# Summing counted edge blocks directly into a ring of three weight tiles, in place of running sums and their differences

## What is computed

```python
# layer 2 (x is already scaled by deg^-1/2)
msg = x[src]
agg = jax.ops.segment_sum(msg, dst, num_segments=h.shape[0])
...
# layer 3 (a self loop is added to the edges)
out = jax.ops.segment_sum(norm[:, None] * h[src], dst, num_segments=N) + b
```

## Time and profile before

| what | us |
|---|---|
| median of 3 timed runs | 4976.39 (4974.26 to 4980.61) |
| the profiled execution, whole | 4979.84 |
| its span, first to last instruction | 4977.6 |
| TensorE busy | 4160.5 (84%) |
| VectorE busy | 2661.7 (53%) |
| ScalarE busy | 1549.6 (31%) |
| GpSimd busy | 1840.2 (37%) |
| mean granted TensorE clock | 0.919 |

### The profile page before, as it was taken

How to read it: one execution, slowest core, us unless ns; L and a number is a source line. 1 busy time by engine, 2 the same in 40 slices (tenths; PEclk the granted TensorE clock), 3 DMA queues, 4 the chain that set the end, 5 groups by cost and what they waited for, 6 DMA issues and landing times. The chain is left out here.

```text
span 4977.6 us, 70703 instructions
## 1 busy us (share of the span) xinstructions
PE 4160.5 (84%) x21605; PEld 3198.6 (64%) x21605; DVE 2661.7 (53%) x5828; ACT 1549.6 (31%) x3042; POOL 1840.2 (37%) x1628
## 2 busy tenths in 40 slices
PE   4899995864917999889999668997799999979978
PEld 2565653643715666568888657886687767768855
DVE  4588888888138999836665560002433322233354
ACT  0233331011314333345565324443001333310023
POOL 0477773872446767536666402113100000000011
PEclk9899997986968999999999879998899999999989
DMA  1599994830845666647666419996423000022200
GB/s 66 177 286 287 295 281 141 260 98 26 264 145 166 181 181 182 190 149 204 184 180 170 138 44 338 323 323 189 122 74 88 1 1 1 2 82 77 61 14 26
DMA packets 519774, 748.78 MB, mean 150 GB/s; under 512 B 80123, under 2 KB 438273, under 8 KB 519301
## 3 DMA queue, kind: packets, MB, share of 16 engines
q1 hardware_dynamic: 405810, 490.95, 31.9%
q0 software_dynamic: 62656, 189.33, 13.8%
q10 hardware_dynamic: 50960, 64.09, 3.7%
HBM read 526.98 MB, written 217.19 MB: 150 GB/s over the span
## 5 line engine op out<-in xcount | busy, mean ns | idle before, releaser
L2828 PE MATMUL sum_ps<-table_rows,block_weights 128*125 128x256 f32 x2500 | 564.7, 386 | 37.1 <-DMA table_rows<-k_table 37.1
L2828 PEld LDWEIGHTS sum_ps<-table_rows,block_weights 128*125 128x125 f32 x2500 | 465.6, 189 | 136.2 <-issue 70.2
L109 POOL DMA_INDIRECT rows_all<-kv_table,src_of_visit x416 | 445.1, 1070 | 221.6 <-issue 111.8
L2632 POOL TENSOR_TENSOR window_sums<-window_sums,brought_blocks 128x650 f32<-128x650 f32 x320 | 427.8, 1337 | 223.6 <-ACT running_blocks L2642 140.2
L2521 POOL DMA_INDIRECT gathered_rows<-k_table,src_of_chunk x392 | 409.2, 1044 | 208.4 <-issue 113.9
L2743 PE MATMUL sum_ps<-gathered_rows,hit 128*126 x1376 | 364.6, 390 | 22.6 <-DVE window_sums L2709 19.0
L2810 DVE TENSOR_TENSOR block_weights<-raw 128x625 f32<-128x625 uint16 x248 | 183.6, 805 | 349.7 <-PE sum_ps L2828 323.6
L2570 PE MATMUL block_ps<-cell_hot,low_hot 128*128 128x325 bf16 x1280 | 231.8, 304 | 141.5 <-DVE cell_hot L2560 140.4
L2057 DVE TENSOR_TENSOR y<-out_ps,b 128x256 f32<-128x256 f32 x120 | 51.0, 425 | 553.0 <-PE out_ps L1956 553.0
L3327 POOL MEMSET eps<- 125x1 f32 x1 | 0.1, 98 | 917.8 <-POOLq L2770 917.8
L2579 ACT ACTIVATE block_copies<-block_ps 128x650 bf16<-128x650 f32 x320 | 227.9, 712 | 358.1 <-PE block_ps L2570 356.7
(11 more groups left out here) (500 smaller groups left out, 8245.8 us busy)
## 6 DMA issues: line engine op xcount, KB each, us to landing
w<-in_L_ffn_W SPq DMA_DIRECT2D x112, 1024.0 KB, 7.5
v_kept<-rows_all SPq DMA_DIRECT2D x104, 512.0 KB, 5.0
v_rows<-v_kept SPq DMA_DIRECT2D x104, 512.0 KB, 4.5
visit_blocks<-block_copies ACTq DMA_DIRECT2D x320, 162.5 KB, 2.9
brought_blocks<-visit_blocks SPq DMA_DIRECT2D x320, 162.5 KB, 3.3
blocks<-running_blocks SPq DMA_DIRECT2D x320, 162.5 KB, 3.5
raw<-blocks SPq DMA_DIRECT2D x250, 162.5 KB, 2.2
w<-in_L_ffn_w SPq DMA_DIRECT2D x64, 256.0 KB, 3.7
```

What stands on the lines that cost most here:

```text
L109: pool.indirect_dma_start(env.ring[:, k % KEPT_RING, i, :], None, env.kv_table, bass.IndirectOffsetOnAxis(env.src_of_visit[:, k * VB + i:k ...
L2632: pool.tensor_tensor(self.totals[:, k % 2, :], self.totals[:, (k - 1) % 2, :], self.brought[:, k % self.BROUGHT, :], ALU.add).then_inc(sel ...
L2828: mm = pe.matmul(sum_ps[0:P, t % banks, 0:D], weights[0:k, t % floats, h, :], rows[0:k, h, :], start=h == 0, stop=h == BH - 1)
```

## The change

The running sums are gone from the attention phase. In each later sum SyncE now brings all 320 counted bf16 blocks in order, eight in flight, and VectorE adds each block in place to the 25 columns of its window in one of three f32 weight tiles: `here * same + block`, where `same` is 1 if the visit has the same window as the one before and 0 if a window begins (so the old contents are dropped). Which tile and which columns, VectorE reads from packed words, one for four visits, that setup now makes with a vector `block_same`; the address of each addition is worked out in registers. TensorE waits for the number of visits up to the end of its tile (`visits_upto`). In the second sum ScalarE copies the result to `part`, and GpSimd adds it. The attention's two kinds of small transfers move from ScalarE's list to SyncE's, one of its tiles gets a buffer of its own, and 17 groups instead of 15 stay in SBUF.

```diff
 setup_phase
-                done(v.tensor_scalar(env.block_last[0:1, 0:BC - 1], bank[6][0:1, 1:BC], -1.0, None, ALU.add))
-                done(v.memset(env.block_last[0:1, BC - 1:BC], BV - 1))
+                done(v.tensor_copy(env.visits_upto[0:1, 0:BC - 1], bank[6][0:1, 1:BC]))
+                done(v.memset(env.visits_upto[0:1, BC - 1:BC], BV))
+                done(v.memset(block_same[:, 0:1], 0.0))
+                done(v.tensor_tensor(block_same[:, 1:BV], tile_bc[1][:, 1:BV], tile_bc[1][:, 0:BV - 1], ALU.is_equal))
+                divided(block_tile, 205, 10)
+                divided(block_lap, 137, 11)
...
 relation_attention_phase
-        running = RunningBlocks(env, st, ph, carve(2 * BX))
...
-                running.sync(sp)
+                for g in range(NS):
+                    if g < NS - KEPT:
+                        bring_back(g)
+                    sp.wait_ge(o_made, g + 1)
+                    n = windows_of(g) * WN
+                    sp.dma_start(env.o_table[g * SW * WN:g * SW * WN + n, :], o_rows[g % 2][0:n, :]).then_inc(stored[g % 2], 16)
...
-                running.gpsimd(pool)
...
-                    exps(g)
-                    running.scalar(act)
+                    exps(g)
...
 dense_sum_phase
-                    at = sp.value_load(env.block_last[0:1, w:w + 1], min_val=0, max_val=BV - 1)
-                    sp.dma_start(raw[:, w % raws, :], env.blocks[ds(at, 1)].rearrange("o p n -> p (o n)")).then_inc(raw_landed[w % raws], 16)
+                    if n >= raws:
+                        sp.wait_ge(added, n - raws + 1)
+                    sp.dma_start(raw[:, n % raws, :], env.visit_blocks[n]).then_inc(raw_landed[n % raws], 16)
...
-                        if w == 0:
-                            ins = v.tensor_copy(block_of, upto(w))
-                        else:
-                            ins = v.tensor_tensor(block_of, upto(w), upto(w - 1), ALU.subtract)
-                        ins.then_inc(converted, 1)
+                v.memset(weights[:, 0], 0.0).then_inc(cleared, 1)
+                v.wait_ge(cleared, 2)
+                v.wait_ge(same_landed, 16)
+                for g in range(BV // BGROUP):
+                    word = v.value_load(env.block_words[0:1, g:g + 1], min_val=1 << 5 * BGROUP, max_val=(T + 1 << 5 * BGROUP) - 1)
+                    laps = [((word >> (5 * i + 3)) & 3).with_bounds(min_val=0, max_val=floats - 1) for i in range(BGROUP)]
+                    places = [((word >> (5 * i)) & 7).with_bounds(min_val=0, max_val=per_tile - 1) for i in range(BGROUP)]
+                    v.wait_ge(multiplied, (word >> (5 * BGROUP)).with_bounds(min_val=1, max_val=T))
+                    for i in range(BGROUP):
+                        n = g * BGROUP + i
+                        v.wait_ge(raw_landed[n % raws], 16 * (n // raws + 1))
+                        if n > 0:
+                            v.wait_ge(added, n)
+                        here = weights[:, ds(laps[i], 1), :, ds(places[i], 1), :].rearrange("p f h o d -> p (f h) (o d)")
+                        v.scalar_tensor_tensor(out=here, in0=here, scalar=same[:, n:n + 1],
+                                               in1=raw[:, n % raws, 0:BH * BW].rearrange("p (h d) -> p h d", h=BH),
+                                               op0=ALU.mult, op1=ALU.add).then_inc(added, 1)
...
+                    upto = pe.value_load(env.visits_upto[0:1, last:last + 1], min_val=1, max_val=BV)
...
+                    pe.wait_ge(added, upto)
...
+                pool.memset(weights[:, 1:floats], 0.0).then_inc(cleared, 1)
+                if onto:
+                    for t in range(T):
+                        pool.wait_ge(taken, t + 1)
+                        pool.tensor_tensor(sums[0:P, t, :], sums[0:P, t, :], part[:, t % 2, :], ALU.add).then_inc(onto_made, 1)
```

More of the change, by code:

```diff
@@ L56 @@
 BCHUNKS = 2
+FLOATS = 3
+BGROUP = 4
 BV = QUADS * (CHUNKS // BCHUNKS) + BC - 1
@@ L2589, in all_stored @@
             act.wait_ge(self.stored[s], 16 * len(range(s, beyond, self.COPIES)))
[L2592 to L2643, removed]
@@ L2762, in dense_sum_phase @@
         rows = sb(env, st, "table_rows", [128, BH, D])
-        raw = sb(env, st, "raw", [128, raws, BX], U16)
-        weights = sb(env, st, "block_weights", [128, floats, BH, P])
+        raw = sb(env, st, "raw", [128, raws, BX], BF16)
+        weights = sb(env, st, "block_weights", [128, floats, BH, per_tile, BW])
+        same = sb(env, st, "block_same", [128, BV])
+        part = sb(env, st, "part_sums", [P, 2, D])
         sum_ps = ps(env, st, "sum_ps", [128, banks, 512])
@@ L2767, in dense_sum_phase @@
         rows_landed = [ph.sem() for _ in range(G + 1)]
-        converted, multiplied, taken = [ph.sem() for _ in range(3)]
+        cleared, same_landed, added, multiplied, taken, onto_made = [ph.sem() for _ in range(6)]
         parts = [(j * G, min(whole, (j + 1) * G)) for j in range(G)]
@@ L2786, in _ @@
                 sp.dma_start(rows[0:N - whole * 128, whole, :], table[whole * 128:N, :]).then_inc(rows_landed[G], 16)
-                for w in range(per_tile, BC):
-                    bring(w)
+                for n in range(raws, BV):
+                    bring(n)
             @block.vector
             def _(v):
-                def upto(w):
-                    return raw[:, w % raws, 0:BH * BW].rearrange("p (h d) -> p h d", h=BH)
-                def take(t):
-                    v.wait_ge(multiplied, t + 1)
-                    here = sums[0:P, t, :]
-                    v.tensor_tensor(here, here, sum_ps[0:P, t % banks, 0:D], ALU.add).then_inc(taken, 1)
@@ L2800, in _ @@
-                for t in range(T):
-                    if t >= floats:
-                        v.wait_ge(multiplied, t - floats + 1)
-                    for i in range(per_tile):
-                        w = t * per_tile + i
-                        v.wait_ge(raw_landed[w % raws], 16 * (w // raws + 1))
-                        block_of = weights[:, t % floats, :, i * BW:(i + 1) * BW]
-                        if w == 0:
-                            ins = v.tensor_copy(block_of, upto(w))
-                        else:
-                            ins = v.tensor_tensor(block_of, upto(w), upto(w - 1), ALU.subtract)
-                        ins.then_inc(converted, 1)
-                    if onto and t >= floats:
-                        take(t - floats)
@@ L2814, in _ @@
-                if onto:
-                    for t in range(T - floats, T):
-                        take(t)
+                v.memset(weights[:, 0], 0.0).then_inc(cleared, 1)
[15 more added lines that the diff above has]
+                                               op0=ALU.mult, op1=ALU.add).then_inc(added, 1)
@@ L2827, in _ @@
                         k = 128 if h < whole else N - whole * 128
-                        mm = pe.matmul(sum_ps[0:P, t % banks, 0:D], weights[0:k, t % floats, h, :], rows[0:k, h, :], start=h == 0,
+                        mm = pe.matmul(sum_ps[0:P, t % banks, 0:D], weights[0:k, t % floats, h].rearrange("p i d -> p (i d)"), rows[0:k, h, :], start=h == 0,
                                        stop=h == BH - 1)
@@ L2956, in relation_attention_phase @@
     with ExitStack() as st:
-        parts = [carve(2 * SW * WR) for _ in range(4)]
+        parts = [carve(2 * SW * WR) for _ in range(3)] + [sb(env, st, "k_t", [128, 2 * SW * WR])[:]]
         q_t = [ap.rearrange("p (m j n) -> p m j n", m=2, j=SW) for ap in parts[0:2]]
@@ L3627, in build @@
         env.visit_blocks = nc.dram_tensor("visit_blocks", (BV, 128, BX), BF16).ap()
-        env.blocks = nc.dram_tensor("blocks", (BV, 128, BX), U16).ap()
+        env.block_same = nc.dram_tensor("block_same", (128, BV), F32).ap()
         env.k_table = nc.dram_tensor("k_table", (N, D), F32).ap()
```

104 lines of the change are left out of this document (60 added, 44 removed).

## The result

The changed kernel takes 5333.22 us (median of 4 runs, 5321.42 to 5343.15), the kernel before, measured beside it, 4975.33 (4972.33 to 4980.61): a ratio of 1.0717 (95% interval 1.0691 to 1.0744). It is 7% slower. The profiled execution of the changed kernel took 5339.14 us with a span of 5337.2; against the one before, 4979.84, that is +359.3.

The account below looks back on a forecast made before the run. TensorE was taken to bind the attention stage and later sums, VectorE the sums after the change. Terms -70 + 6 + 182 + 190 = +308 on 4979.84 gave 5288, less 3.4 for the median: 5284 us, range 5145 to 5385.

Parts of the forecast that it names:

- setup: Before the attention stage: a net 18 chained steps at a third of a microsecond each, +6 us, between 3 and 9.
- attention stage: TensorE's wait for the softmax vanishes and groups get shorter: -70 us, lower bound of the gain 46, upper 79.
- first later sum: VectorE's 320 additions take 451 us and become the bound; the sum ends at 4003 against 3821, +182 us.
- second later sum: The same 451 us of additions, plus GpSimd's hold-ups; it ends at 4929.5 against 4739.2, +190 us.
- addition: Later sums: one VectorE addition of a block over 625 columns takes 861 ns.
- pause: Later sums: idle time between two additions, with five register steps in it, 0.55 us, ends 0.27 and 0.77.
- ninth block: First tile of a later sum: this block is queued behind the table's rows, so about 4 us are lost.
- GpSimd's share of the second sum: GpSimd's 25 additions hold up VectorE by up to 0.41 us each: +8 us, and 1 for the last one.
- Rival 1: Later sums: register steps run under the addition before, about 0.90 us an addition, 4958 us in all; chance 0.05.
- Rival 2: Later sums: only part of the register steps shows, a pause of 0.27, 1.13 us a visit, 5105 us; chance 0.08.
- Rival 3: Later sums: TensorE's clock stays low at 1.2 GHz, 22.3 us a tile, 5498 us; chance 0.04.
- Rival 4: Attention stage: it gains nothing because another wait takes the place, 5354 us; chance 0.05.

Follow-up runs that it names:

- e1_steps_ahead: The changed kernel with the wait for the addition before moved from the first register step to the addition itself; 5014.61 us, ratio 1.0072 to the kernel before.
- e3_half_products: The changed kernel with TensorE making only every second product of a tile (13 of 25) in the two later sums; 5320.57 us in one run.
- e7_steps_and_start: The changed kernel with the wait on the addition, ring places numbered through, earlier word load, sixteen blocks in flight, tile clearing shared by three engines; 4949.77 us, ratio 0.9943.
- e5_additions_alone: The kernel before without ScalarE's copies and stores of running totals, but with blocks brought and GpSimd's 320 additions kept; 4964.01 us, ratio 0.9968.
- e4_no_totals: The kernel before without running sums in the attention stage; the later sums subtract the counted blocks themselves; 4898.06 us, ratio 0.9837.

## Why the prediction was right, and where it was off

| term, us | forecast | profiled |
|---|---|---|
| setup | +6 | +6.9 |
| attention stage | -70 | -85.4 |
| first later sum | +182 | +207.7 |
| second later sum | +190 | +216.0 |
| all other stages | 0 | +14 |
| sum | +308 | +359 |

The forecast was 5284 us with a range of 5145 to 5385; 5333 lies in it, on the upper half. The direction and the mechanism were right: VectorE became the bound of the later sums, by the length of one addition and a pause made of register steps behind a wait. The two sums cost 52 us more than forecast. That the total is off by no more than 49 is in part luck: the attention stage gave back 15 more than forecast, and the other stages took 14 more.

- **The addition**, 861 ns worked out from the columns of the earlier trace rows, is 870. The **pause** was taken at 0.55 and is 0.62: this term was mis-sized. It was inside its ends, 0.27 and 0.77, but its sum was made with 57 ns for a fused step, the low end of the earlier trace rows, plus a little for the time between steps; an address with two indices takes 75 to 151 for each. Together a visit costs 1.49 in place of 1.41 us: 0.08 x 640 = 51 us, all that the two sums are longer than forecast (26 + 26).
- **The attention stage** gave back 85.4, more than the upper bound of 79, and a group takes 22.06 us, below the 22.4 to 22.9 named as a sign. That bound came from the one group of the earlier trace rows, 22.44 us without its wait; taking it as the least that a group can need is the step that failed. Why it needs 0.38 more stays open: its timeline shows no other wait of TensorE. Of the 33 us put down to groups below the full clock, a part was something else: the wait for the masks, which the prediction doesn't name, falls from 12.8 to 3.7 us. The rest of that reading holds: the value products behind the softmax (L3065, now L3066) take 22.3 us less in all, and the gathered weights (L3054, now L3055) 36.0 in place of 43.0, with the stage's granted clock at 0.97 in place of 0.93. With the wait of the earlier trace rows, 45.9 to 4.3, this makes 80 of the 85.4. The first row is the wait for the masks in the changed kernel, then come the value products before and after:

```profile
PE score_ps L3044 <- DVE window_sums L3160: 3.7, 2, 2.3
L3065 PE MATMUL v_ps<-composed,window_sums 128*126 128x256 f32 (+1 forms) x600 | 160.5, 432 | 0.0
L3066 PE MATMUL v_ps<-composed,window_sums 128*126 128x256 f32 (+1 forms) x600 | 138.2, 388 | 0.0
```

- **Setup, the start, the ninth block, the last tile and GpSimd's share of the second sum** were right within a few us: the next stage begins 6.9 us later; the first addition of the first sum stands 6.65 us behind the barrier, the ninth visit waits 4.71; the last tile's products take 12.86, and the second sum is 9 us longer than the first (I had 8 and 1):

```profile
3460.71 5.31 POOL L2822 MEMSET block_weights<- 128x6250 f32 x1 [25.59 <-POOLq L1885]
3467.36 0.87 DVE L2787 SCALAR_TENSOR_TENSOR block_weights<-block_weights,block_same,raw 128x625 bf16 x1 [3.27 <-issue]
3483.38 0.87 DVE L2787 SCALAR_TENSOR_TENSOR block_weights<-block_weights,block_same,raw 128x625 bf16 x1 [4.71 <-DMA raw<-visit_blocks]
...
3947.87 12.86 PE L2804 MATMUL sum_ps<-table_rows,block_weights 128*125 128x256 f32 x50 [5.38 <-DVE block_weights L2787]
```

- **All other stages** are 14 us longer in this execution. No term of the change stands there. e1_steps_ahead and e3_half_products are the same program up to the first later sum and reach it at 3447.18 and 3456.10, where this one does at 3460.71. So executions of one program spread over about as much as these 14 us, and the median of the runs lies 6 us below this one.
- **Rival 1** (the steps hide) was rejected for the right reason, the place of the wait. e1_steps_ahead makes it come true with the same steps. The Trainium skill, Perfetto Trace Analysis, section on the DVE / Act engine instruction, lets the sequencer go on once an instruction with its wait is in the wait queue; the 0.037 us between additions in e1_steps_ahead agree. The 0.62 us where a register step carries the wait fit the other reading that the prediction gave, that such a step waits in the sequencer itself. The price of that rival, 4958, was too low for e1_steps_ahead, where the word's load does not hide (5014.61); e7_steps_and_start, where it does hide, takes 4949.77, and its sums are 19.7 and 26.4 us longer than before, as that rival had them (19 and 27). **Rival 2** (a pause of 0.27) falls by the 0.62. **Rival 3** (the clock) falls by the changed kernel's own rows: at a granted clock of 0.81 a tile takes 12.94 us and not 22.3, and TensorE waits 351.7 us for VectorE; e3_half_products adds that with half the products the sums are only 5 to 6 us shorter. **Rival 4** falls by the 588.50.

## What to carry to other kernels

In a chain of short dependent instructions, see on which instruction the wait stands: on the first register step of an address it puts all steps on the path, on the instruction that needs it they are hidden, and here that one move was worth 6%. Price the pause between such instructions with register steps that make an address of the same number of indices. And when an engine that is far from full is freed of work, look for what its operations stretched on another engine, in every group of instructions and not only in the one that ends the longest wait.

## What the runs showed of the hardware

A fused register step took 57 to 64 ns where one index made the address and 75 to 151 ns with two. In e1_steps_ahead and e7_steps_and_start a finished addition lets the next one, waiting for it, start 0.037 us later. Loading a word from SBUF into a register took 304 ns, and the fused step behind it 190 to 205.

In e5_additions_alone against e4_no_totals, GpSimd's additions (430 us of them beside the stage) stretched only VectorE instructions whose two tensor operands both lie in SBUF: on the mean the mixing from 425 to 849 ns, the scaling from 308 to 829 and the subtraction of the maximum, of the scaling's shape, from 308 to only 333, while the mask of the same kind that reads PSUM stayed at 1208. ScalarE's copies and their transfers stretched none of them (VectorE's busy time is 333.87 us with and without them). The Trainium skill, SBUF — State Buffer, section "SBUF: two separate sides", says that a VectorE operation with two SBUF inputs and a GpSimd operation that reads SBUF take a shared port in turns and the later one waits for the whole of the other; the rows agree.
